# Cross attention on one core: output products of 128 tokens across batch borders, 28 in place of 32

## What is computed

```python
a = _layer_norm(audio_kv, ln_gamma, ln_beta)              # (32, 375, 512)
Q = hidden_states @ Wq.T                                  # (32, 112, 512)
K = a @ Wk.T
V = a @ Wv.T                                              # 16 heads of 32
scores = einsum('bhtd,bhsd->bhts', Q, K) * 32 ** -0.5
attn = softmax(where(mask, scores, -inf))
out = einsum('bhts,bhsd->bhtd', attn, V) -> (32, 112, 512)
return hidden_states + tanh(gate) * (out @ Wo.T)
```

## Time and profile before

| | us |
|---|---|
| median of 3 runs | 940.44 (939.95 to 940.76) |
| the profiled execution, its own time | 940.45 |
| its span in the trace | 938.4 |
| PE busy | 928.2 (99% of the span) |
| ACT busy | 685.8 (73%) |
| DVE busy | 706.4 (75%) |
| POOL busy | 639.4 (68%) |
| granted TensorE clock, mean of the core | 1.0 of full speed |

### The profile page before, as it was taken

How to read it: one execution, slowest core, us unless ns; L and a number is a source line. 1 busy time by engine, 2 the same in 40 slices (tenths; PEclk the granted TensorE clock), 3 DMA queues, 4 the chain that set the end, 5 groups by cost and what they waited for, 6 DMA issues and landing times.

```text
span 938.4 us, 26747 instructions
## 1 busy us (share of the span) xinstructions
PE 928.2 (99%) x10723; PEld 805.9 (86%) x10723; DVE 706.4 (75%) x1381; ACT 685.8 (73%) x1296; POOL 639.4 (68%) x724
## 2 busy tenths in 40 slices
PE   9999999999999999999999999999999999999997
PEld 8898888888888888888888888888888888888885
DVE  6972498778777778777877777877787777887677
ACT  3422687777778787787877778777787777878775
POOL 0672366777777777777777777877777777777765
PEclk9999999999999999999999999999999999999999
DMA  9983143334344433444434443344443443334212
GB/s 280 344 266 150 29 101 93 92 104 115 90 98 113 111 92 88 104 113 116 105 85 111 115 107 82 93 111 114 115 98 90 113 114 95 91 94 113 56 39 59
DMA packets 85850, 105.54 MB, mean 112 GB/s; under 512 B 22528, under 2 KB 63488, under 8 KB 85728
## 3 DMA queue, kind: packets, MB, share of 16 engines
q1 hardware_dynamic: 85152, 102.93, 41.3%
q10 hardware_dynamic: 576, 0.92, 0.3%
HBM read 86.39 MB, written 17.43 MB: 111 GB/s over the span
## 4 chain that ended last, share of the span: by engine, by line
PE 95%; DMA 1%; DVE 1%; ACT 1%; SPq 0%; issue 0%; DVEq 0%
PE banks L959 66%; PE banks L1104 10%; PE banks L1117 8%; PE banks L982 7%; PE banks L1123 2%; DMA shared_f<-in_xT 1%; ACT shared_q L630 0%; ACT shared_q L639 0%; DMA x_odd<-row_stats 0%; DVE shared_q L865 0%; PE banks L1085 0%; DVE shared_r L751 0%; PE banks L990 0%; SPq L319 0%; ACT shared_f L644 0%
## 5 line engine op out<-in xcount | busy, mean ns | idle before, releaser
L959 PE MATMUL banks<-shared_r,w_k 128*128 128x376 f32 x1536 | 291.7, 339 | 0.6 <-ACT shared_f L680 0.5
L630 ACT ACTIVATE shared_q<-banks,maskT,rstd 125x448 f32<-125x448 f32 x384 | 243.4, 729 | 55.3 <-PE banks L1104 55.0
L959 PE MATMUL banks<-w_v,shared_r 128*125 128x512 f32 x1152 | 283.5, 395 | 0.0
L855 DVE TRANSPOSE_TENSOR_REDUCE rmax<-shared_q 128x14 f32<-128x448 f32 x384 | 219.8, 625 | 82.3 <-ACT shared_q L630 81.1
L959 PEld LDWEIGHTS banks<-shared_r,w_k 128*128 128x128 f32 x1536 | 263.1, 188 | 13.5 <-issue 0.9
L493 POOL TENSOR_TENSOR shared_f<-shared_q 125x448 f32<-125x448 f32 x124 | 142.0, 1145 | 163.7 <-PE banks L1123 163.2
L959 PEld LDWEIGHTS banks<-w_v,shared_r 128*125 128x125 f32 x1152 | 212.9, 186 | 44.5
L865 DVE TENSOR_TENSOR shared_q<-shared_q,banks 125x448 f32<-125x448 f32 x384 | 208.2, 607 | 0.1
L639 ACT ACTIVATE shared_q<-shared_q 125x448 f32<-125x448 f32 x384 | 186.4, 568 | 2.5 <-DVE shared_q L865 2.5
L497 POOL TENSOR_TENSOR shared_f<-shared_f,shared_q 125x448 f32<-125x448 f32 x124 | 142.3, 1148 | 9.7
L461 POOL TENSOR_TENSOR shared_r<-cn,shared_r 128x375 fp32r<-128x375 f32 x124 | 112.3, 927 | 42.9 <-ACT shared_r L591 42.8
(11 more groups left out here) (93 smaller groups left out, 785.1 us busy)
## 6 DMA issues: line engine op xcount, KB each, us to landing
cn<-in_ctxT SPq DMA_DIRECT2D x128, 187.5 KB, 4.0
rows<-in_ctx SPq DMA_DIRECT2D x32, 720.0 KB
xy<-in_x SPq DMA_DIRECT2D x32, 224.0 KB, 7.4
q_kept<-shared_q SPq DMA_DIRECT2D x8, 896.0 KB, 7.5
shared_q<-q_kept SPq DMA_DIRECT2D x32, 224.0 KB, 3.9
out<-xy SPq DMA_DIRECT2D x32, 224.0 KB, 3.8
shared_f<-in_xT SPq DMA_DIRECT2D x7, 896.0 KB, 11.3
x<-row_stats SPq DMA_DIRECT2D x64, 84.0 KB
```

Source lines behind the costliest of these rows:

```text
L630: act.activation(prob[0:SP_, n % NB, j, :] .rearrange("p (a h t) -> p a h t", a=2, h=2), score_view(n, j), ACT.Identity, bias=maskT[0:SP_, ...
L855: last = dve.tensor_reduce(rmax[:, n % 2, BLK * j:BLK * j + BLK], prob[:, n % NB, j, :].rearrange("p (k a) -> p k a", a=32), AX.X, ALU.max ...
L959: last = pe.matmul(dst, l, m, start=(start and k == 0), stop=(stop and k == len(pairs) - 1))
```

## The change

The 32 batches of 112 tokens are 3584 tokens, which is 28 tiles of 128. The high and low parts of the normalised tokens go into a ring of 256 token columns, batch after batch, and an output product takes 128 columns of the ring, whichever batches they come from. `tile_of(b)` is the tile whose last tokens come with batch b: none for b = 0, 8, 16 and 24 (those batches complete no tile), else b - 1 - b // 8. So the calls that stood for batch c - 3 now stand for tile `tile_of(c - 3)`, and are left out for c = 3, 11, 19 and 27. `pieces(b)` cuts the copy of a batch at the ring's end: it gives two pieces for b = 2, 4, 6, 9, 11, 13, 18, 20, 22, 25, 27 and 29, one for the others. Row blocks of x and of the result have 128 rows, and `gated`, `gbo` and the output bank use 128 partitions.

```diff
+TILES = B * T // 128
+RING = 256
...
-        XR = 4 * KT * GN
+        XR = 4 * KT * GN + 9 * 128
...
-        at, oT = cut_r(at, 2, KT, T)
+        at, oT = cut_r(at, 2, KT, RING)
...
-            return oT[:, a, 2 * i:2 * i + 2, :].rearrange("p c t -> p (c t)")
+            at = (B - 1) * T % RING
+            return oT[:, a, 2 * i:2 * i + 2, at:at + T]
...
+        def tile_of(b):
+
+            return b - 1 - b // 8 if 0 <= b < B and b % 8 else None
...
+        def tiles(b):
+
+            return b - b // 8 if b > 0 else 0
+
+        def pieces(b):
+
+            at = b * T % RING
+            n = min(T, RING - at)
+            return [(0, at, n)] + ([(n, 0, T - n)] if n < T else [])
+
+        def sums_of(b):
+            return pv[:, b % 2 * HT:b % 2 * HT + HT].rearrange("p (c t) -> p c t", c=KT)
 
...
+            def load_x(t):
+                need(sync, stored[t % XB], t // XB * 16)
+                sync.dma_start(xy[:, t % XB, :], x_rows[128 * t:128 * t + 128, :]) \
+                    .then_inc(ld_x[t % XB], 16)
+
+            def store(t):
+                sync.wait_ge(y_done, t + 1)
+                sync.dma_start(out_rows[128 * t:128 * t + 128, :], xy[:, t % XB, :]) \
+                    .then_inc(stored[t % XB], 16)
...
-                    if c > 3:
-                        store(c - 4)
+                    if tile_of(c - 4) is not None:
+                        store(tile_of(c - 4))
                     if QB <= c + 2 < B:
                         load_q(c + 2)
-                if odd and XB <= c < B:
-                    load_x(c)
-            for b in range(B - 4, B):
-                store(b)
+                if odd and tile_of(c) is not None and tile_of(c) >= XB:
+                    load_x(tile_of(c))
...
             def low_half(b):
                 pool.wait_ge(o_hi, b + 1)
-                pool.tensor_tensor(oT[:, 1, :, :].rearrange("p c t -> p (c t)"),
-                                   pv[:, b % 2 * HT:b % 2 * HT + HT],
-                                   oT[:, 0, :, :].rearrange("p c t -> p (c t)").bitcast(F32),
-                                   ALU.subtract).then_inc(o_done, 1)
+                for t, at, n in pieces(b):
+                    last = pool.tensor_tensor(oT[:, 1, :, at:at + n], sums_of(b)[:, :, t:t + n],
+                                              oT[:, 0, :, at:at + n].bitcast(F32), ALU.subtract)
...
-                    if c > 2:
-                        add_bias(c - 3)
-                if odd and c > 2:
-                    result(c - 3)
+                    if tile_of(c - 3) is not None:
+                        add_bias(tile_of(c - 3))
+                if odd and tile_of(c - 3) is not None:
+                    result(tile_of(c - 3))
...
-                need(act, y_mm, b)
-                act.activation(oT[:, 0, :, :].rearrange("p c t -> p (c t)"),
-                               pv[:, b % 2 * HT:b % 2 * HT + HT], ACT.Copy).then_inc(o_hi, 1)
-
-            def gated_out(b, at=VO):
-                act.wait_ge(y_mm, b + 1)
-                need(act, y_done, b)
-                act.activation(gated[0:T, :], bank[at][0:T, :], ACT.Copy, scale=gat[0:T, 0:1]) \
+                need(act, y_mm, (b * T - RING + T - 1) // 128 + 1)
+                for t, at, n in pieces(b):
+                    last = act.activation(oT[:, 0, :, at:at + n], sums_of(b)[:, :, t:t + n], ACT.Copy)
+                last.then_inc(o_hi, 1)
+
...
-                if odd and 3 <= c < B - 1:
-                    gated_out(c - 3)
+                if odd and c < B - 1 and tile_of(c - 3) is not None:
+                    gated_out(tile_of(c - 3))
...
-                if j == 0 and c > 3:
-                    pe.wait_ge(y_out, c - 3)
-                elif b == VO:
-                    need(pe, v_done, c * ST + j)
-                product(bank[b][0:SP_, :],
+                if j == 0:
+                    need(pe, y_out, tiles(c - 4))
+                need(pe, v_done, c * ST + j)
+                product(bank[VO][0:SP_, :],
                         [(cT[:, c % 2, d, k, SP_ * j:SP_ * j + SP_], wv[:, a, k, :])
...
-                product(bank[at][0:T, :],
-                        [(oT[:, a, k, :], wo[:, d, k, :])
+                at_row = 128 * tile_of(b) % RING
+                product(bank[at],
+                        [(oT[:, a, k, at_row:at_row + 128], wo[:, d, k, :])
                          for k in range(KT) for a, d in PASSES]).then_inc(y_mm, 1)
...
-                            last = pe.matmul(bank[1][0:T, :], oT[:, a, k, :], wo[:, d, k, :],
+                            last = pe.matmul(bank[1], oT[:, a, k, RING - 128:RING], wo[:, d, k, :],
...
-                if odd and 3 <= c < B - 1:
+                if odd and c < B - 1 and tile_of(c - 3) is not None:
                     output(c - 3, c * ST + ST)
```

More of the change, by code:

```diff
@@ L387, in _ @@
                 if not odd:
[L388 to L389 removed]
+                    if tile_of(c - 4) is not None:
+                        store(tile_of(c - 4))
                     if QB <= c + 2 < B:
                         load_q(c + 2)
[L392 to L395 removed]
+                if odd and tile_of(c) is not None and tile_of(c) >= XB:
+                    load_x(tile_of(c))
+            for t in range(tiles(B - 5), TILES):
+                store(t)
             for k in range(XB):
[L397 removed]
+                sync.wait_ge(stored[k], 16 * (TILES // XB))
         @block.gpsimd
@@ L463, in context_lo, with add_bias, result @@
                     .then_inc(c_done, 1)
-            def add_bias(c):
-                pool.wait_ge(ld_x[c % XB], (c // XB + 1) * 16)
-                pool.tensor_tensor(xy[0:T, c % XB, :], xy[0:T, c % XB, :], gbo[0:T, :], ALU.add) \
+            def add_bias(t):
+                pool.wait_ge(ld_x[t % XB], (t // XB + 1) * 16)
+                pool.tensor_tensor(xy[:, t % XB, :], xy[:, t % XB, :], gbo[:, :], ALU.add) \
                     .then_inc(xb_done, 1)
[L470 to L473, removed]
+            def result(t):
+                pool.wait_ge(xb_done, t + 1)
+                pool.wait_ge(y_out, t + 1)
+                pool.tensor_tensor(xy[:, t % XB, :], xy[:, t % XB, :], gated[:, :], ALU.add) \
                     .then_inc(y_done, 1)
@@ L549, in _ @@
                 slot_pair(m)
-            add_bias(B - 3)
+            add_bias(TILES - 3)
             normalised(B - 2)
             low_half(B - 2)
-            result(B - 3)
-            add_bias(B - 2)
-            add_bias(B - 1)
+            result(TILES - 3)
+            add_bias(TILES - 2)
+            add_bias(TILES - 1)
             pool.wait_ge(last_hi, 1)
-            pool.tensor_tensor(pair_of(1, 0), last_half(0), pair_of(0, 0).bitcast(F32),
+            pool.tensor_tensor(pair_of(1, 0), last_pair(0), pair_of(0, 0).bitcast(F32),
                                ALU.subtract).then_inc(last_done[0], 1)
-            result(B - 2)
+            result(TILES - 2)
         @block.scalar
@@ L613, in _ @@
             act.wait_ge(bo_mm, 1)
-            act.activation(gbo[0:T, :], bo_bank[0:T, :], ACT.Copy, scale=gat[0:T, 0:1]) \
+            act.activation(gbo[:, :], bo_bank, ACT.Copy, scale=gat[:, 0:1]) \
                 .then_inc(bo_out, 1)
@@ L654, in high_half, with gated_out @@
                 act.wait_ge(o_norm, b + 1)
-                need(act, y_mm, b)
-                act.activation(oT[:, 0, :, :].rearrange("p c t -> p (c t)"),
-                               pv[:, b % 2 * HT:b % 2 * HT + HT], ACT.Copy).then_inc(o_hi, 1)
-            def gated_out(b, at=VO):
-                act.wait_ge(y_mm, b + 1)
-                need(act, y_done, b)
-                act.activation(gated[0:T, :], bank[at][0:T, :], ACT.Copy, scale=gat[0:T, 0:1]) \
+                need(act, y_mm, (b * T - RING + T - 1) // 128 + 1)
+                for t, at, n in pieces(b):
+                    last = act.activation(oT[:, 0, :, at:at + n], sums_of(b)[:, :, t:t + n], ACT.Copy)
+                last.then_inc(o_hi, 1)
+            def gated_out(t, at=VO):
+                act.wait_ge(y_mm, t + 1)
+                need(act, y_done, t)
+                act.activation(gated[:, :], bank[at], ACT.Copy, scale=gat[:, 0:1]) \
                     .then_inc(y_out, 1)
@@ L741, in _ @@
             exponential(SLOTS - 1)
-            gated_out(B - 2)
+            gated_out(TILES - 2)
             last_high(0)
@@ L900, in last_low @@
                 dve.wait_ge(last_hi, i + 1)
-                dve.tensor_tensor(pair_of(1, i), last_half(i), pair_of(0, i).bitcast(F32),
+                dve.tensor_tensor(pair_of(1, i), last_pair(i), pair_of(0, i).bitcast(F32),
                                   ALU.subtract).then_inc(last_done[i], 1)
             def last_result():
[L905 to L909, removed]
+                dve.wait_ge(xb_done, TILES)
+                dve.wait_ge(y_mm, TILES)
+                dve.wait_ge(y_done, TILES - 1)
+                y = xy[:, (TILES - 1) % XB, :]
```

(3 more changed lines are left out.)

23 lines of the change are left out of this document (11 added, 12 removed).

## The result

The changed kernel takes 932.13 us (median of 4 runs, 931.33 to 933.48) against 940.6 us before: a ratio of 0.9911, interval 0.9894 to 0.9928. A second set of five runs took 932.21 us (0.9913, 0.9900 to 0.9927). That is 8.4 us gained.

A forecast was written before the change was run, and what follows sets the result against it. PE, busy for 928.2 of 938.4 us, was taken as the bound, with ACT setting the pace in pairs without an output product. Sum: 940.45 - 6.20 + 0.2 + 0.1 = 934.55, forecast 934.6 us, range 932.4 to 937.1.

The forecast's parts named there:

- Four products go, each a pair of 11.54 us: Odd pairs at c = 3, 11, 19, 27 fall from 13.09 to 11.54 us, 6.20 us gained in all.
- ACT sets the pace there, with two waits of half a microsecond: Odd pairs without output product: PE waits for ACT's copies of K (0.57 us) and of the weighted sums (0.54 us).
- The second piece of the high half, 0.11 us each: ACT's split high half at c = 11 and 27, on its path there: 0.2 us lost in all.
- The bound of 2.5 us: Upper bound on the four pairs' loss if each run of 112 in ACT's high half cost like its own instruction.
- The last store, 0.1 us: End of the kernel: a last store of 256 KB in place of 224 KB adds 0.1 us, at most 0.3.
- The high half elsewhere: ACT in pairs with an output product: 1.01 us of slack covers the split high halves, zero cost.
- the new waits on PE: `project_v(c, 0)` waiting for two copies out of bank 7, and the ring's overwriting rule: zero cost.
- POOL, SP: POOL's changed calls and SP's 28 loads and stores in place of 32: POOL zero, SP nothing besides the last store.
- The whole gain: Rival: each of the four pairs gives the product's full 2.89 us, 928.9 us in all; chance 0.05.
- the slower case: Rival: ACT's copies into the ring become the bound in odd pairs, for example 950.4 us; chance 0.03.
- The other 28 products: Remaining output products, with 128 weight columns in place of 112: no change in pitch taken, at worst 4.4 us lost.
- the loss that a sum of both would give: Rival: the wider weight load adds its 13 ns to each output product matmul, 4.4 us, giving 939.0; chance 0.06.

The follow-up runs named there:

- skip4: Kernel before the change, with only the output products of batches 0, 8, 16 and 24 left out, products keeping 112 weight columns: 934.16 us, 0.9933.
- high_early: Changed kernel with ACT's high half moved ahead of the copy of K in five odd pairs without an output product: 930.54 us, 0.9898.
- vsplit: On high_early, V's third product cut into 8 and 4 matmuls around the second K product in six odd pairs without an output product: 927.93 us, 0.9867.
- v384: Changed kernel with V's weight loads at 128 columns and the context's four parts of 128 channels 384 elements apart: 933.17 us, 0.9917.
- vchunk: Changed kernel with 128 context columns for each V chunk, all V loads 128 wide from multiples of 512 bytes, K reading 3 x 126 columns: 931.75 us, 0.9906.
- stride128: Kernel before the change, with each batch given 128 columns of oT but only the 112 that hold tokens loaded as weights: 941.27 us, 1.0006.
- shift32: Changed kernel with the ring 32 elements (128 bytes) further on in memory: 934.25 us, 0.9934.
- shift64: Changed kernel with the ring 64 elements (256 bytes) further on in memory: 932.14 us, 0.9912.

## Why the prediction was right and wrong

- *Four products go, each a pair of 11.54 us.* Right: 11.54 us at c = 3 and 19, in the changed kernel and in skip4. The early pair of batch 2 was the case itself.
- *ACT sets the pace there, with two waits of half a microsecond.* Right: the changed trace has them, and high_early removed the one for the copy of the weighted sums and vsplit the one for the copy of K. DVE's 11.47 of 11.54 us was no bound.
- *The second piece of the high half, 0.11 us each.* 0.09 us. The four runs of 112 with a step cost nothing: the copy of 448 elements takes 568 ns as before. The bound of 2.5 us was not needed.
- *The last store, 0.1 us.* Too small to tell: from the last pair's start to the end of the span there are 36.0 us before, and 36.1 and 35.6 in two profiles of the changed kernel.
- *The high half elsewhere, the new waits on PE, POOL, SP.* Right at zero; no such wait shows.
- *The whole gain, the slower case.* Neither came.
- *The other 28 products.* **This is the step that failed.** It read: "A wider load does not show in the pitch. I take nothing; if the 13 ns were in series, it would be 28 x 12 x 13 = 4.4 us." I bounded it on the side of a loss alone, because I reckoned with the load's own time; the pitch in fact falls, by 6 ns a matmul, 28 x 12 x 6 = 2.0 us. The reason I gave, that 112 and 125 columns run at the same pitch, is true, but both are on the slow side of what decides. The step needed both ends, and no reason excluded a gain: the rows of before had no stream with loads of 128 columns beside 512 moving ones. The nearest streams in that trace, K's and Q's, have such loads with 376 and 448 moving columns and take 172 and 205 ns from start to start; a straight line through them gives, as an estimate, 234 ns at 512, so they would not have shown the gain either. With the measured term the sum is 934.55 - 2.0 = 932.5 us, 0.4 us from the median.
- *The rule of the Trainium skill on loads* (TensorE: Matmul & The Clock Gate, "LDWEIGHTS (loading the stationary operand)"), time by columns, holds for the difference between the loads, 175 and 188 ns. Their size it does not give: by the rule they would take 93 and 107 ns, an estimate from it, and the trace has some 81 ns more in both. It does not carry over to the pitch, and no run here shows the loss that a sum of both would give.

## What to carry to other kernels

When work is taken off the busiest engine, look for a place in the trace where that work is already missing: the pairs ahead of the first output product gave the price of the gap to a hundredth of a microsecond, where the work's own time was off by a factor of 1.9. What a gap gives back is then a matter of order: here the work that had covered ACT's copies was gone, and moving one copy ahead and cutting one product brought 4.2 us more. And a change in the shape or the address of a matmul's weights needs a bound on both sides. Moving a tile for one product's sake can cost another: in v384 and vchunk the gain of V was largely lost in K and in the output product.

## What the runs showed of the hardware that I had not expected

A matmul of 512 fp32r columns, in a stream where each has its own weight load, takes 241 ns by busy time over count (227 from start to start) when the load has 128 columns at the ring's place in the changed kernel, and 247 to 248 ns (232 to 234) when it has 112 columns at such addresses (stride128) or 128 columns 128 bytes further on (shift32); 256 bytes further on it is 241 ns again (shift64). The load's own time doesn't show it: 188 ns in the fast and in the slow case of 128 columns. The Trainium skill (TensorE: Matmul & The Clock Gate, "Weight-path perf modes — Fast Weight Load (FWL) and DoubleRow") has a faster load for exactly 128 weights of a type other than FP32; the width agrees with what is seen here, but the loads of 128 columns take no less time than the column rule says, so these runs do not show that it is this mode.
